# First feed-forward: maximum over the parts in two halves around the next chunk's `hidden`, with the convolution of two parts ahead of turning it

## The reference

```
def act_quant(x):    scale = 127 / clip(max(|x|, axis=-1), 1e-5);  return clip(round(x * scale), -128, 127) / scale
def weight_quant(w): scale = 1 / clip(mean(|w|), 1e-5);            return clip(round(w * scale), -1, 1) / scale
h = bit_linear(layernorm(x), w1)             # 128 -> 512, both operands quantized
h = silu(depthwise_conv1d(h over the 64 tokens of a sequence, width 3, padding 1))
x = x + bit_linear(h, w2)                    # 512 -> 128, both operands quantized
```

## Time and profile before

| | |
|---|---|
| median of 3 runs | 1141.4 us (1141.16 to 1143.77) |
| the profiled execution | 1140.98 us, its span 1139.3 us |
| mean granted TensorE clock | 0.747 |
| busy share PE / PEld / DVE / ACT / POOL | 65% / 48% / 65% / 36% / 33% |
| first feed-forward, from PE's first work at 127.4 to the barrier | to 218.7 us |

### The profile page before, as it was taken

How to read it: one execution, slowest core, us unless ns; L and a number is a source line. 1 busy time by engine, 2 the same in 40 slices (tenths; PEclk the granted TensorE clock), 3 DMA queues, 4 the chain that set the end, 5 groups by cost and what they waited for, 6 DMA issues and landing times. The chain is left out here.

```text
span 1139.3 us, 21553 instructions
## 1 busy us (share of the span) xinstructions
PE 745.4 (65%) x7849; PEld 549.4 (48%) x7859; DVE 746.2 (65%) x2331; ACT 410.7 (36%) x789; POOL 377.4 (33%) x470
## 2 busy tenths in 40 slices
PE   4887578366666959343799255539799999922322
PEld 2555334245454937322689234225678777711111
DVE  4798486599994246565488556674365556549985
ACT  3787532143333034231133142415344444332221
POOL 3563799133344031047244200010022121224544
PEclk9899699655555559555899757759899999975555
DMA  8400000011100031011644200000000000000000
GB/s 307 176 2 2 0 1 1 2 53 55 44 1 1 2 68 25 1 51 50 191 152 160 91 1 1 0 1 0 1 2 3 3 2 2 3 1 0 10 9 19
DMA packets 23418, 42.54 MB, mean 37 GB/s; under 512 B 2658, under 2 KB 13507, under 8 KB 22580
## 3 DMA queue, kind: packets, MB, share of 16 engines
q1 hardware_dynamic: 21044, 36.50, 9.6%
q0 software_dynamic: 2272, 4.69, 1.3%
HBM read 22.56 MB, written 8.40 MB: 27 GB/s over the span
## 5 line engine op out<-in xcount | busy, mean ns | idle before, releaser
L3031 POOL TENSOR_TENSOR l3x_probs<-l3x_E,l3x_inv 128x1024 f32<-128x1024 f32 x16 | 30.9, 1932 | 101.9 <-DVE l3x_inv L3070 101.9
L362 ACT ACT_TABLE_LOAD x9 | 11.5, 1283 | 142.2 <-PEq L151 142.2
L3056 DVE TENSOR_REDUCE l3x_top<-l3x_p_s 128x8 f32<-128x512 f32 x32 | 20.6, 686 | 58.7 <-PE l3x_p_s L2902 58.7
L2045 POOL DMA_INDIRECT moe_replies<-l1gb_inbox x39 | 38.1, 976 | 57.2 <-DVE l1gb_inbox L2180 52.9
L2134 ACT ACTIVATE l1gb_hidden<-l1gb_hidden 128x512 f32<-128x512 f32 x39 | 24.6, 630 | 75.6 <-DVE l1gb_hidden L2166 71.4
L2091 PE MATMUL l1gb_p_h<-l1gb_xT,l1gb_w_now 128*128 128x128 f32 x312 | 44.8, 289 | 6.6 <-issue 5.0
L961 PE MATMUL l0f_p_h<-l0f_hpad,l0f_taps 128*128 128x512 f32 x96 | 46.9, 638 | 0.0
L680 POOL TENSOR_TENSOR l0x_kspread<-l0x_kT,l0x_groupmask 128x512 f32<-128x512 f32 x32 | 32.7, 1042 | 41.4 <-ACT l0x_kT L604 41.4
L2091 PEld LDWEIGHTS l1gb_p_h<-l1gb_xT,l1gb_w_now 128*128 128x128 f32 x312 | 39.5, 199 | 11.0 <-issue 9.3
L3393 PE MATMUL l3fb_p_h<-identity_bf,l3fb_hq 128*128 128x128 bf16 x64 | 8.3, 310 | 55.6 <-DVE l3fb_hq L3331 55.6
L2100 PE MATMUL l1gb_p_y<-params_l1w,l1gb_hidden 128*128 x312 | 41.1, 276 | 0.7 <-ACT l1gb_hidden L2134 0.7
(11 more groups left out here) (657 smaller groups left out, 2406.0 us busy)
## 6 DMA issues: line engine op xcount, KB each, us to landing
l1gb_w_now<-params_l1w SPq DMA_DIRECT2D x39, 256.0 KB
params_l1w<-in_l1w SPq DMA_DIRECT2D x2, 2048.0 KB, 12.0
l_toeplitz<-s4d_lags SPq DMA_DIRECT2D x64, 64.0 KB
moe_slots<-l1f_blank SPq DMA_DIRECT2D x1, 2535.0 KB, 15.6
l1gb_inbox<-moe_slots SPq DMA_DIRECT2D x9, 260.0 KB, 5.2
params_l3x<-in_l3x SPq DMA_DIRECT2D x1, 2048.0 KB, 22.1
l1g_rows<-moe_replies SPq DMA_DIRECT2D x8, 256.0 KB, 4.9
params_l2x<-in_l2x SPq DMA_DIRECT2D x1, 1028.5 KB, 16.0
```

The source lines that it names most:

```text
L2045: pool.indirect_dma_start(moe.replies[:, :], bass.IndirectOffsetOnAxis(inbox[:, j, D:D + 1].bitcast(I32), 0), outbox[:, j, :], None).then_ ...
L3031: pool.tensor_tensor(Pn[:], E[:], wide(inv[:].rearrange("p a j -> p j a").unsqueeze(3), [P, J, 2, S]), ALU.mult)\
```

## The change

PE's `first` is split into `first_input` (turning `xq`, spreading `deq1`) and `first` (the four products). In PE's list of a chunk, the parts 0 and 1 now stand ahead of `turn_top` of the chunk before, part 2 between that and `spread_up`, and part 3 and `first_input` of the next chunk ahead of `second`. DVE's `highest` is given the half of the chunk's tokens that it treats (256 of 512); the first half is done where the whole was, the second half behind `hidden` of the next chunk, and the output of the chunk before follows both. `turn_top` waits for both halves.

```diff
--- before.py
+++ after.py
@@ -917,13 +917,15 @@
                         last = pe.matmul(out[:, i, :], wide(column[:, i:i + 1], [P, P]), core.ident[:], start=True, stop=True)
                     last.then_inc(done, 1)
 
-                def first(c):
+                def first_input(c):
                     pe.wait_ge(xq_ready, c + 1)
                     for i in range(TC):
                         last = pe.transpose(p_x[:, i, :], xq[:, i, :], core.ident_bf[:])
                     last.then_inc(x_turned, 1)
                     pe.wait_ge(deq1_ready, c + 1)
                     spread(p_spread, deq1, spread1_done)
+
+                def first(c):
                     pe.wait_ge(xqT_ready, c + 1)
                     if c == 0:
                         pe.wait_ge(wq_ready, 1)
@@ -933,7 +935,7 @@
                         pe.matmul(p_h[:, k, :], wq1[:, k * P:(k + 1) * P], xqT[:], start=True, stop=True).then_inc(h_done, 1)
 
                 def turn_top(c):
-                    pe.wait_ge(top_ready, c + 1)
+                    pe.wait_ge(top_ready, 2 * c + 2)
                     for i in range(TC):
                         last = pe.transpose(p_top[:, i, :], top[:, i * P:(i + 1) * P], core.ident[:])
                     last.then_inc(top_turned, 1)
@@ -962,19 +964,22 @@
                                          hpad[:, k, :, side:side + S], start=(side == 0), stop=(side == 2))
                     last.then_inc(conv_done, 1)
 
+                first_input(0)
                 first(0)
                 pe.wait_ge(taps_ready, 1)
                 for c in range(NC):
+                    convolved(c, 0)
+                    convolved(c, 1)
                     if c:
                         turn_top(c - 1)
-                    convolved(c, 0)
+                    convolved(c, 2)
                     if c:
                         spread_up(c - 1)
-                    convolved(c, 1)
-                    convolved(c, 2)
+                    convolved(c, 3)
+                    if c + 1 < NC:
+                        first_input(c + 1)
                     if c:
                         second(c - 1)
-                    convolved(c, 3)
                     if c + 1 < NC:
                         first(c + 1)
                 turn_top(NC - 1)
@@ -1053,11 +1058,12 @@
                         dve.wait_ge(y_done, c)
                     dve.tensor_scalar(hq[:], gc[:], ROUND, ROUND, ALU.add, ALU.subtract).then_inc(hq_ready, 1)
 
-                def highest(c):
+                def highest(c, half):
+                    ns = slice(half * CH // 2, (half + 1) * CH // 2)
                     dve.wait_ge(g_ready, c * K + K)
                     if c:
                         dve.wait_ge(top_turned, c)
-                    dve.tensor_reduce(top[:], g[c % 2][:].rearrange("p k n -> p n k"), AX.X, ALU.max, apply_absolute_value=True)\
+                    dve.tensor_reduce(top[:, ns], g[c % 2][:, :, ns].rearrange("p k n -> p n k"), AX.X, ALU.max, apply_absolute_value=True)\
                         .then_inc(top_ready, 1)
 
                 quantized_weights(0, "w1T", wq1[:])
@@ -1066,17 +1072,20 @@
                 dve.wait_ge(pads_ready, 1)
                 hidden(0)
                 quantized(1)
-                highest(0)
+                highest(0, 0)
                 hidden(1)
+                highest(0, 1)
                 for c in range(NC):
                     hidden_peak(c)
                     if c + 2 < NC:
                         quantized(c + 2)
                     hidden_quantized(c)
                     if c + 1 < NC:
-                        highest(c + 1)
+                        highest(c + 1, 0)
                     if c + 2 < NC:
                         hidden(c + 2)
+                    if c + 1 < NC:
+                        highest(c + 1, 1)
                     output(c)
 
             @block.scalar
```

## The result

| | before | after |
|---|---|---|
| median of 6 runs | 1141.68 us (1140.23 to 1145.11) | 1133.19 us (1131.09 to 1134.86) |
| ratio, 95% interval | | 0.9916 (0.9901 to 0.9931) |
| the profiled execution, its span | 1140.98, 1139.3 us | 1131.25, 1129.5 us |
| start of the first maximum to the end of the stage's last statistics, **S** | 142.81 to 218.68: 75.87 us | 140.94 to 207.30: 66.36 us |
| ahead of S, behind S | 142.8, 920.6 us | 140.9, 922.2 us |

The forecast was 1133.5 us. The kernel is 8.5 us faster by the medians. In the profiled pair S explains 9.5 of 9.8 us: the code ahead of and behind S is the same in both, and its time differs by -1.9 and +1.6 us.

A forecast was written before the change was run, and what follows sets the result against it. Bound by a ring of waits among DVE, ACT and PE in the first feed-forward, no engine full. Terms -4.2 - 4.8 + 0.2 + 0.1 + 0.55 + 0.3 = -7.85, taken as -7.9: median 1133.5 us, range 1130.5 to 1139.0.

The forecast's parts named there:

- first period: First maximum to the second: 18.0 us taken against 17.78, 0.2 worse; sums 17.3 without and 18.6 with a stall.
- second period: Maximum of chunk 1 to that of chunk 2: links through ACT's rounding and SiLUs sum to 16.4 against 20.63, -4.2.
- third period: Next maximum to the last: links through spreading, scaling `g` and rounding sum to 16.1 against 20.88, -4.8.
- tail: From the last maximum on: two halves +0.1, `up2` beside GpSimd +0.55, PE's `turn_top` at the lower clock +0.3.
- Half a maximum at 1.92 us: DVE's `top` of 3.71 us, halved with about 0.13 fixed; bounds 1.85 and 3.7, cost +0.1 us a chunk.
- `second`'s wait for `hq`: PE's `second` needs `hq` after 5.1 us but has 4.9 of other work: a wait of 0.2.
- rival 5: `hidden` held anyway by `first`: margin 0.4 us; if gone, loss some 0.3 a chunk, -7; inside the forecast's 0.68.
- The bounds: Whole change: -9.5 us with every stall at its lower end, about -6 with every one at its upper.
- The clock: PE's longest idle time within a chunk near 1.1 us, before part 0, so full clock expected and dips vanish.
- the dip was half hidden: Before, part 0 ran at 1.2 GHz, a dip of 1.75 us; PE waited 1.13 us for `up2` afterwards.
- The slower rival: Parts 0 and 1 of chunks 1 to 3 at 1.2 GHz, 1.75 us each: +2.6, median 1144; chance 0.06.
- the ring: First feed-forward: DVE waits for ACT, ACT for PE, PE for DVE; periods before 17.78, 20.63 and 20.88 us.

The follow-up runs named there:

- e3: The change with both halves of the maximum one behind the other ahead of `hidden`; S 77.34 us, not timed.
- e8: The change with ACT's SiLUs of parts 0 and 1 ahead of raising and rounding the next inputs; S 65.19 us, ratio 0.9924 to before.
- e7: The change with GpSimd's table left out and its result set to zero, so the output differs; S 64.57 us, not timed.
- e11: e8 with the output of chunk 2 moved behind the peaks of chunk 3; S 64.95 us, ratio 0.9917 to before.
- e10: The change itself run again, unaltered; S 66.47 us, ratio 0.9916 to before.
- e4: The change with `second` back in its old place between parts 2 and 3; S 82.98 us, not timed.
- e5: The kernel before with 18 matmuls whose result nobody reads behind `first`, to hold PE's clock up; S 77.71 us, ratio 1.0003 to before.
- e2: The change's PE order alone, with the maximum in one piece ahead of `hidden`; S 77.12 us, ratio 0.9990 to before.
- e9: e2 with 21 matmuls whose result nobody reads behind `first`, to hold PE's clock up; S 71.65 us, ratio 0.9968 to before.
- e1: The change's two halves alone, with PE's list as it was before; S 81.91 us, ratio 1.0063 to before.
- e12: e11 with matmuls whose result nobody reads in PE's three waits of the tail; S 64.11 us, ratio 0.9901 to before.
- e6: The change with `turn_top` behind part 0 instead of behind part 1; S 67.59 us, not timed.

## Why the prediction was right, by its steps

| term | predicted | measured in S |
|---|---|---|
| first period | +0.2 | -0.52 |
| second period | -4.2 | -4.06 |
| third period | -4.8 | -5.07 |
| tail | +0.95 | +0.14 |
| sum | -7.85 | -9.51 |

- **Half a maximum at 1.92 us**: 1.93 to 1.96 us; e3 prices the split at 0.2 us over four chunks. Right. (The row of 0.67 us that its sum uses stands in the earlier trace rows, not in rows 7.)
- **Second period closed by ACT**: the sum of links 16.4, measured 16.57, with each link within 0.1 us. e8 confirms the link: with the SiLUs first DVE does not wait for them.
- **Third period closed by spreading, scaling and rounding**: 16.1 said, 15.81 measured; `up2` took 0.17 us, and the rounding 1.61.
- **First period**: here I put half a GpSimd operation for a stall of the small operations. They were not hit (0.18 and 0.22 us); the rounding was (1.88 us), beside ACT's SiLUs. The no-stall sum was 17.3, the measured one 17.26. The term was mis-sized by 0.7.
- **Tail**: 0.55 for a stalled `up2`. GpSimd hit `deq2` right behind it instead (1.23 us at 197.32), and PE's spreading covered that. The 0.3 for `turn_top` at the lower clock came (1.12 against 0.66 us) but ended before DVE's output did, so it cost nothing. Mis-sized by 0.8. The Trainium skill's rule that I cited ("SBUF — State Buffer", "Who interferes with whom") agrees with e7, but which operation it hits could not be told from the sum: in e11 it was `up2`. It is not chance from one execution to the next either: in e10 the same operations of the changed kernel were hit (`up2` 1.07, rounding 1.98, `deq2` 1.23 us).
- **`second`'s wait for `hq`**: 0.2 said, 0.55, 0.16 and 1.45 us measured, the last without a `first` behind it. That the old place would be ruinous was not in the text; e4 shows it.
- **`hidden` held by `first`** (rival 5): it did not come, but the margin is thin. In the second period PE had `first` done at 159.7 us and `hidden` began at 160.05, when the half was done.
- **The bounds**: the text gives -9.5 "with every stall at its lower end" and about -6 at the upper. From its own terms they come out at -9.1 (-9.4 with `turn_top` at full clock) and -6.5. Nor is the lower one free of stalls: the 1.89 us of the second period hold an `up2` of 0.97, and e7, with none at all, has an S of 64.57, 11.3 below before. That S fell by just 9.5 is a coincidence.
- **The clock**: full clock said and seen. But "the dip was half hidden" was too little. PE still waited 1.13 us for `up2` behind it, so all 1.75 us lay in time that PE would have waited anyway, and e5 shows this. And the expectation of e2 held the halves to be worth half a maximum, 1.86 us, a period. They are worth more in this order: from e2 (77.1) to the change (66.4) is 10.8 us, of which e9 (71.65) gives 5.5 to the clock and 5.3 to DVE's time. The 5.3 holds GpSimd's stalls of two different kernels, so it is good to about 1 us. The slower rival was real, only one edit away: with the whole maximum PE idles 2.8 us before part 0 in two of three periods and runs part of the pair at 1.2 GHz; with half it idles 1.05 us and does not.

By the medians the gain, 8.5 us, lies between the predicted 7.9 and the 9.5 of S; the rest of the kernel moves by a few us from execution to execution, and I did not trace where. So the mechanism is borne out by the periods, but that the median came within 0.3 us of the forecast is in part luck: the stage gained 1.7 us more than the sum said.

What stays open: what exactly brings the clock down. In the three periods of the changed kernel PE waits 1.07 us at most and there is no dip. Dips came behind waits of 2.2 us in before, 2.8 us in e2 and 4.7 us in e1. But a wait of 2.2 us in the first period of before stood in a stretch at 1.00, and behind 2.31 us in e2, 2.89 us in e5 and 2.60 us in e11 PE's next work still ran at full clock. So the length of the one wait before it doesn't decide alone.

The wait in the first period of before:

```profile
146.57 0.66 PE L938 MATMUL l0f_p_top<-identity,l0f_top 128*128 128x128 f32 x4 [2.22 <-DVE l0f_top L1060]
147.16 2.84 PE L961 MATMUL l0f_p_h<-l0f_hpad,l0f_taps 128*128 128x512 f32 x6
```

## What to carry to other kernels

Walk the ring of the new order link by link, with durations from the trace, and through every engine's list: which engine closes it changed from period to period here, and the sum of a period came out within 0.3 us wherever no stall was guessed. Halving an operation pays when it stands between two engines, and only if the other engine's order uses it; here each edit alone gave nothing or a loss, and both gave 9.5 us of S. When an experiment puts a longer wait in front of TensorE, look at the granted clock before the duration is believed, and hold it up with a filler to separate the two.

## What the runs showed of the hardware

- Two waits of PE of 2.8 us were each followed by the granted clock at 0.50 and a pair of parts at 7.1 and 8.2 us instead of 5.4 (e2). Waits of 2.31 us (e2) and 2.89 us (e5) were followed by a pair at 5.42 and 5.32 us, at 1.00. Matmuls with a result that nobody reads, put into the wait, kept the clock at 1.00 (e5 at 166 us, e9 in its three periods, e12 in the tail until 205.0).
- A `tensor_scalar` of 4 elements takes 0.17 to 0.23 us with GpSimd idle (e7) and up to 1.31 us (e8) beside GpSimd's operations of 1.26 us; the rounding of 2048 elements takes 1.23 and up to 2.25 us (e6). Half a maximum takes 1.9 us either way.
- The maximum over the four parts, read with the part innermost (2048 elements to 512), takes 3.7 us and its half 1.93, against 2.29 for 2048 elements to one: the time goes by elements or outputs, not by instruction. Which of the two was not separated, nor what the order of reading costs.
